# Attention on half arrays: probability-times-value and projection matmuls split into two 64-row matmuls, and the second pair's projection started in query block 4

## The reference, cut to what matters

```python
q, k, v = split(x @ c_attn_kernel.T + c_attn_bias)         # 16 heads of 64
w = softmax(q @ k.T / 8, causal)                           # per head
x = layernorm(x + (w @ v) @ c_proj_kernel.T + c_proj_bias)
h = gelu(x @ w1 + b1)                                      # 4096 wide
x = layernorm(x + h @ w2 + b2)
```

## Time and profile before

| | us |
|---|---|
| median of 3 runs | 2371.99 (2371.93 to 2372.07) |
| the profiled execution, its own time | 2373.32 |
| its span on the slowest core (core 5) | 2371.7 |
| spans of all cores | 2354.2 to 2371.7 |
| mean granted TensorE clock of the cores | 0.986 to 0.993 |

### The profile page before, as it was taken

How to read it: one execution, slowest core, us unless ns; L and a number is a source line. 1 busy time by engine, 2 the same in 40 slices (tenths; PEclk the granted TensorE clock), 3 DMA queues, 4 the chain that set the end, 5 groups by cost and what they waited for, 6 DMA issues and landing times.

```text
span 2371.7 us, 47143 instructions; the slowest of 8 cores (2354.2 to 2371.7 us)
## 1 busy us (share of the span) xinstructions
PE 2185.2 (92%) x20126; PEld 1328.4 (56%) x20126; DVE 774.7 (33%) x1925; ACT 1369.8 (58%) x1666; POOL 218.0 (9%) x181
## 2 busy tenths in 40 slices
PE   7997998999999989989878799999999999999997
PEld 3553654545545455445444466666666666666665
DVE  3434434344333343443412132222223322222221
ACT  2794788998999989999999222222222222222222
POOL 2000000000000000000111311111111111111110
PEclk8999999999999999999899899999999999999999
DMA  9500100001000000000392511100111111111000
GB/s 146 88 15 3 28 8 13 13 6 28 8 6 21 6 17 11 6 11 8 83 169 47 109 45 45 44 20 27 45 45 45 45 45 45 45 45 45 19 8 30
DMA packets 52554, 88.57 MB, mean 37 GB/s; under 512 B 3200, under 2 KB 35968, under 8 KB 51328
## 3 DMA queue, kind: packets, MB, share of 16 engines
q0 software_dynamic: 16784, 33.56, 9.2%
q1 hardware_dynamic: 35568, 52.00, 6.6%
HBM read 93.94 MB, written 25.17 MB: 50 GB/s over the span
## 4 chain that ended last, share of the span: by engine, by line
PE 80%; ACT 8%; DVE 8%; DMA 2%; issue 2%; POOL 0%; POOLq 0%; SPq 0%; DVEq 0%
PE ps L794 18%; PE ps L776 18%; PE ps L270 12%; PE ps L434 11%; PE ps L481 8%; ACT work L450 8%; PE ps L363 5%; PE ps L625 4%; DVE qkv L281 4%; DVE work L811 2%; PE ps L300 2%; DMA qkv<-w 1%; DVE stat L304 1%; PE ps L514 1%; PE ps L668 1%
## 5 line engine op out<-in xcount | busy, mean ns | idle before, releaser
L450 ACT ACTIVATE work<-ps,cb 128x1024 bf16<-128x1024 f32 (+3 forms) x1152 | 1123.3, 1059 | 158.8 <-PE ps L434 152.4
L784 ACT ACTIVATE work<-ps,b_s 128x256 bf16<-128x256 f32 x512 | 243.8, 476 | 794.7 <-PE ps L776 794.7
L794 PE MATMUL ps<-qkv,work 128*128 128x512 bf16 x2048 | 526.7, 380 | 21.3 <-DVE work L811 20.9
L776 PE MATMUL ps<-work,xT 128*128 128x256 bf16 x4096 | 533.2, 273 | 1.5 <-DVE work L518 1.5
L776 PEld LDWEIGHTS ps<-work,xT 128*128 128x128 bf16 x4096 | 401.9, 98 | 158.3 <-issue 2.3
L481 PEld LDWEIGHTS ps<-qkv,work 128*128 128x128 bf16 x8448 | 395.0, 98 | 157.1 <-issue 34.0
L434 PE MATMUL ps<-qkv 64*128 64x512 bf16 (+3 forms) x2304 | 432.2, 370 | 42.4 <-ACT work L450 37.7
L481 PE MATMUL ps<-qkv,work 128*128 128x65 bf16 x8448 | 440.9, 194 | 3.0 <-DVE work L500 2.2
L270 PE MATMUL ps<-xT,work 128*128 128x512 bf16 x1024 | 340.3, 386 | 54.5 <-DVE qkv L281 50.2
L794 PEld LDWEIGHTS ps<-qkv,work 128*128 128x128 bf16 x2048 | 198.3, 98 | 209.7 <-issue 31.1
L270 PEld LDWEIGHTS ps<-xT,work 128*128 128x128 bf16 x1024 | 79.5, 97 | 210.8 <-issue 197.6
(11 more groups left out here) (42 smaller groups left out, 744.4 us busy)
## 6 DMA issues: line engine op xcount, KB each, us to landing
work<-x SPq DMA_DIRECT2D x16, 1024.0 KB, 5.1
out<-work SPq DMA_DIRECT2D x16, 1024.0 KB, 4.0
attn_s<-work SPq DMA_DIRECT2D x64, 128.0 KB, 1.7
xT<-w POOLq DMA_DIRECT2D x8, 1024.0 KB, 14.9
work<-attn_s SPq DMA_DIRECT2D x16, 512.0 KB, 6.3
qkv<-w POOLq DMA_DIRECT2D x16, 512.0 KB, 9.3
xT<-xb POOLq DMA_DIRECT2D x7, 1024.0 KB, 45.5
work<-wqk POOLq DMA_DIRECT2D x7, 512.0 KB, 6.1
```

The costliest lines, as they stand in the source:

```text
L450: lambda: sc.activation(pb, ps, AF.Exp, bias=cb[:, 8 * p + g : 8 * p + g + 1], scale=0.125),
L776: r = t.matmul(bank(4 + ui % 2)[:, 0:TB], w1[:, FF * f + 128 * hc : FF * f + 128 * hc + 128], x2T[b % 2][:, TB * f : TB * f + TB], start=f ...
L784: lambda: sc.activation(hbuf[ui % 4], bank(4 + ui % 2)[:, 0:TB], AF.Gelu, bias=b1[:, hc : hc + 1]),
L794: r = t.matmul(bank(2 * c + oh), hbuf[ui % 4][:, 128 * c : 128 * c + 128], w2[hc][:, 512 * oh : 512 * oh + 512], start=hc == 0, stop=hc == 31)
```

## The change

1. `put_values` becomes `put_half`, run twice for a unit. The first takes rows 0 to 63 (keys) for one head and rows 64 to 127 for the other, alternating, with bank 6 and 7 each written from one half of the array. The second takes the other rows for each head ("exchanged"). So 8 matmuls of 128 rows become 16 of 64 rows. `run_halves` puts the first half before the next scores and the second behind them; the second waits on TensorE's own semaphore for the first. Where nothing stands between, halves are held back (`order[1]`).
2. The fill projections for pairs 1 to 7 become `qk_pairs` and `v_pairs`: 16 steps of two 64-row matmuls, one to bank 4 and one to bank 5, rows exchanged after step 7, so that query and key block (or two value tiles) are computed at once. Step 8 waits for step 7; `run_fill` stops after step 7. Pair 0's own projections stay as they were.
3. Costs get `GAP = 3.0` credits before a group and before the two norm sums, which now run together (`norm_pair`).
4. Pair 1's projections start in block 4 of pair 0: one block of them in `g = 4`, one in 5, two in 6, four in 7. The rate is the sum of costs over `4g + 3` units.
5. `turn_block` is held back while banks 4 and 5 are open.

```diff
+    def two_tiles(lhs0, rhs0, out0, lhs1, rhs1, out1, start, stop, after, mark):
+        def go():
+            x = t.matmul(out0, lhs0, rhs0, start=start, stop=stop, skip_group_check=True)
+            y = t.matmul(out1, lhs1, rhs1, start=start, stop=stop, skip_group_check=True)
+            return x, y
+        return pe.put(go, *after, mark=mark)
+
+    def qk_pairs(p, g):
...
+                turned, fc = divmod(n, 8)
...
+                qi0, qi1 = (1, 0) if turned else (0, 1)
...
+                tok = two_tiles(
+                    w[0:64, o0 : o0 + 128], xT[0:64, xs], bank(4 + qi0),
+                    w[64:128, o1 : o1 + 128], xT[64:128, xs], bank(4 + qi1),
+                    n == 0, n == 15,
+                    (gb_free[0], gb_free[1], ld_qk[p], ld_x[g]) if n == 0 else (st.get(7),) if n == 8 else (),
+                    n in (7, 15))
...
+        return [(1.0 + (GAP if n == 0 else 0.0), step(n)) for n in range(16)]
+
+    def norm_pair(p, g):
...
+        return [(3.0 + GAP, go)]
+
+    def v_pairs(vp, a):
...
+        return [(0.5 + (GAP if n == 0 else 0.0), step(n)) for n in range(16)]
+
+    def next_qk(p, lo, hi):
+        out = []
+        for g in range(lo, hi):
+            out += qk_pairs(p, g) + norm_pair(p, g)
+        return out
...
+    def run_halves():
+        while halves and (halves[0][1] or order[1]):
+            i, first = halves.popleft()
+            if not first:
+                order[0] = 1 - order[0]
+            put_half(i, order[0], first)
+            order[1] = False
...
-            for h in range(2):
-                o = 260 * j + 65 * (2 * (p % 2) + h)
-                for c in range(max(0, j - 4 * g), 4):
+            for c in range(max(0, j - 4 * g), 4):
+                for half in range(2):
+                    h = half ^ swap
+                    o = 260 * j + 65 * (2 * (p % 2) + h)
+                    rows = slice(64 * half, 64 * half + 64)
                     r = t.matmul(bank(6 + h)[:, 65 * c : 65 * c + 65],
-                                 pbuf[i % NP][:, 512 * h + 128 * c : 512 * h + 128 * c + 128],
-                                 w[:, o : o + 65], start=j == 0 and c == 0, stop=j == 4 * g + c,
-                                 skip_group_check=True)
+                                 pbuf[i % NP][rows, 512 * h + 128 * c : 512 * h + 128 * c + 128],
+                                 w[rows, o : o + 65], start=first and j == 0 and c == 0,
+                                 stop=not first and j == 4 * g + c, skip_group_check=True)
...
-            go()
+            order[1] = True
+            if go() and not all_:
+                break
...
-                    rate[0] = 34.0 / (4 * g + 3)
-                else:
-                    fill.extend(next_steps(0))
-                    rate[0] = sum(c for c, _ in fill) / 28.0
+                lo, hi = {4: (0, 1), 5: (1, 2), 6: (2, 4), 7: (4, 8)}.get(g, (0, 0))
+                fill.extend(next_qk(1, lo, hi))
+                rate[0] = sum(c for c, _ in fill) / (4 * g + 3)
...
-        if p == 0 and g == NG - 1 and j == 28:
-            run_fill(all_=True)
+        run_halves()
...
             put_scores(i + 1)
         t_p[i] = put_exp(i)
+        run_halves()
...
-            put_values(waiting.popleft())
+            queue_values(waiting.popleft())
...
-        while turns and i - turns[0][0] >= 5:
+        while turns and i - turns[0][0] >= 5 and not gb_open[0] and not gb_open[1]:
```

More of the change, by code:

```diff
@@ L23 @@
 NP = 7
+GAP = 3.0
 NB = S // TB
@@ L252, in build_nc @@
     sq_free = [None, None]
+    t_sq = [None, None]
     sq_next = [0]
@@ L398, in qkv0, with step, go @@
         return work
+    def two_tiles(lhs0, rhs0, out0, lhs1, rhs1, out1, start, stop, after, mark):
[5 more added lines that the diff above has]
+    def qk_pairs(p, g):
+        w = wqk[p % 2]
+        st = {}
+        def step(n):
+            def go():
+                turned, fc = divmod(n, 8)
+                if n == 0:
+                    gb_open[0] = gb_open[1] = True
+                qi0, qi1 = (1, 0) if turned else (0, 1)
+                o0 = 1024 * qi0 + 128 * fc
+                o1 = 1024 * qi1 + 128 * fc
+                xs = slice(S * fc + QB * g, S * fc + QB * g + QB)
+                tok = two_tiles(
[4 more added lines that the diff above has]
+                    n in (7, 15))
+                st[n] = tok
+                if n == 15:
+                    for qi in range(2):
+                        dst = (q2, k2)[qi][p % 2][:, QB * g : QB * g + QB]
+                        gb_free[qi] = t_qk[p, qi, g] = dve.put(
+                            lambda qi=qi, dst=dst: v.tensor_scalar(
+                                dst, bank(4 + qi), bqk[:, 8 * qi + p : 8 * qi + p + 1], None, ALU.add),
+                            tok, ld_bqk, q2_done.get(p - 2))
+                    for qi in range(2):
+                        src = (q2, k2)[qi][p % 2][:, QB * g : QB * g + QB]
+                        t_sq[qi] = dve.put(lambda qi=qi, src=src: v.tensor_mul(sq[qi], src, src),
+                                           t_qk[p, qi, g], sq_free[qi])
+                    wqk_done[p] = tok
+                    gb_open[0] = gb_open[1] = False
+                return n == 7
+            return go
+        return [(1.0 + (GAP if n == 0 else 0.0), step(n)) for n in range(16)]
@@ new lines, in norm_pair, with go @@
+    def norm_pair(p, g):
+        def go():
+            for qi in range(2):
+                tok = pe.put(lambda qi=qi: t.matmul(bank(4 + qi), ones, sq[qi], start=True, stop=True),
+                             t_sq[qi], t_ones, gb_free[qi])
+                sq_free[qi] = tok
+                c = 16 * p + 8 * qi + g
+                gb_free[qi] = t_rd[p, qi, g] = dve.put(
+                    lambda qi=qi, c=c: v.reduce_max(stat[:, c : c + 1], bank(4 + qi), axis=AX.X), tok)
+            bound(p, g)
+        return [(3.0 + GAP, go)]
@@ new lines, in v_pairs, with step, go @@
+    def v_pairs(vp, a):
+        w = wv[vp % 2]
+        st = {}
+        def step(n):
+            def go():
+                turned, fc = divmod(n, 8)
+                if n == 0:
+                    gb_open[0] = gb_open[1] = True
+                b0, b1 = (1, 0) if turned else (0, 1)
+                c0, c1 = (S * fc + 128 * (a + b0), S * fc + 128 * (a + b1))
+                ws = slice(256 * fc, 256 * fc + 256)
+                tok = two_tiles(
+                    xT[0:64, c0 : c0 + 128], w[0:64, ws], bank(4 + b0)[:, 0:256],
+                    xT[64:128, c1 : c1 + 128], w[64:128, ws], bank(4 + b1)[:, 0:256],
+                    n == 0, n == 15,
+                    (gb_free[0], gb_free[1], ld_v[vp], ld_x[a // 4]) if n == 0 else (st.get(7),) if n == 8 else (),
+                    n in (7, 15))
+                st[n] = tok
+                if n == 15:
+                    for b in range(2):
+                        gb_free[b] = t_v[vp, a + b] = dve.put(
+                            lambda b=b: v.tensor_tensor(
+                                va[vp % 2].rearrange("p (a h c) -> p a h c", a=NKT, h=4)[:, a + b, :, 0:64],
+                                bank(4 + b)[:, 0:256].rearrange("p (h c) -> p h c", h=4),
+                                bvb[:, 256 * vp : 256 * vp + 256].rearrange("p (h c) -> p h c", h=4),
+                                ALU.add),
+                            tok, ld_bv, va_done.get(vp - 2))
+                    wv_done[vp] = tok
+                    gb_open[0] = gb_open[1] = False
+                return n == 7
+            return go
+        return [(0.5 + (GAP if n == 0 else 0.0), step(n)) for n in range(16)]
@@ L400, in next_steps @@
+    def next_qk(p, lo, hi):
[3 more added lines that the diff above has]
+        return out
     def next_steps(p):
+        tiles = {1: (1, 0, 32), 2: (2, 0, 16), 3: (2, 16, 32), 4: (3, 0, 16), 5: (3, 16, 32)}
         out = []
-        if p + 1 < NPAIR:
-            out += joined([qk_block(p + 1, g) for g in range(NG)])
-        tiles = {1: (1, 0, 32), 2: (2, 0, 16), 3: (2, 16, 32), 4: (3, 0, 16), 5: (3, 16, 32)}
         if p in tiles:
@@ L407, in next_steps @@
             vp, lo, hi = tiles[p]
-            vs = [s for a in range(lo, hi) for s in v_steps(vp, a)]
-            out = vs + out
+            for a in range(lo, hi, 2):
+                out += v_pairs(vp, a)
+        if p + 1 < NPAIR:
+            out += next_qk(p + 1, 0, NG)
         return out
@@ L468, in build_nc, with queue_values, put_half @@
     attN_free = [None] * 2
-    def put_values(i):
+    halves = deque()
+    order = [0, False]
+    first_half = {}
+    def queue_values(i):
+        halves.extend([(i, True), (i, False)])
+    def run_halves():
[5 more added lines that the diff above has]
+            order[1] = False
+    def put_half(i, swap, first):
         p, g, j = units[i]
@@ L744, in build_nc @@
         while waiting and i - waiting[0] >= hold:
-            put_values(waiting.popleft())
+            queue_values(waiting.popleft())
```

(10 more changed lines are left out.)

7 lines of the change are left out of this document (6 added, 1 removed).

## The result

The changed kernel is slower: its median is 2388.36 us, against 2371.99 before. Two of its five executions fell in the chip's slow state (2614 and 2622 us), so the ratio is of the undisturbed executions alone: 1.0053, with a 95% interval of 1.0037 to 1.0069. The forecast was 2317 with a range up to 2355, so it was wrong in sign.

A forecast was written before the change was run, and what follows sets the result against it. Exponentials on ScalarE were taken to bound pairs 6 and 7, TensorE the others. Pairs 2 to 5 -36, pair 1 -12, pair 0 -5, pair 6 -0.5: -53.5, called -55, from 2372 to 2317 us; range 2272 to 2355.

The forecast's parts named there:

- What bounds the kernel: Attention: exponentials on ScalarE bound pairs 6 and 7, TensorE decides elsewhere; only time above 141 us per pair can be won.
- Price of a side-by-side pair of short matmuls: Values in halves: two 65-column matmuls side by side taken at 0.036 us, bounds 0.029 to 0.058.
- no overlap: Rival: short value matmuls don't overlap, 0.058 us per pair, +106 us, 2478; chance 0.16, whole or in part.
- the rule that the prediction cites beside it: Value halves: some 60 cycles overhead per matmul, so sixteen short matmuls would take eight's time once more.
- The wait between the halves: Each unit: second value half waits for the first behind the next scores; 0.09 us left open, bounds 0 and 0.2.
- Load per unit: TensorE in attention: 0.62 us per unit against 0.66, up to 0.07 of waits less; with fill 0.84, 0.94, 1.04.
- From load to time: Pair times from load: a tenth of a microsecond worth 12 to 16 us per pair, below about 0.9 nothing.
- Transposes may come some units later, and nobody waits for them: Attention: stores follow transposes that may come some units later, and nobody waits for them inside attention.
- Pairs 6 and 7 at "-0.5" and "0": Pair 6, already at the exponentials' bound, would change by -0.5 us, and pair 7 by 0.
- Evictions and gaps: Fill: gaps of three credits, over a microsecond, take away most waits of 5.7 + 1.7 + 1.4 + 1.2 us.
- Pair 0 (-5): Pair 0: block 7 -32 us, blocks 4 to 6 +6, +6.5, +9.5, blocks 1 to 3 +5; in sum -5.
- Given back: Rival: pair gains eaten by pair 0's packed blocks and TensorE's stalls on its own semaphore (0.2); about 2370, chance 0.07.

The follow-up runs named there:

- both edits: Changed kernel with transposes put ahead of the fill and values whole (128 rows) in pair 7; 2360.52 us, ratio to before 0.9939.
- credit by width: Changed kernel with transposes ahead of fill, pair 7 values whole, and pairs 1 to 7 credit following each unit's exponential width; 2351.09 us, ratio to before 0.9897.
- all four edits: Changed kernel with transposes ahead of fill, values whole in pairs 7 and 0, credit by the width of the unit; 2341.37 us, ratio to before 0.9857.
- The early start alone: Kernel before, with only pair 1's projections (128 rows as before) begun in block 4 of pair 0; 2365.26 us, ratio 0.9964.
- late loads: Changed kernel with feed-forward weights loaded from block 7 of pair 7, not its start; blocks 0 to 6 took 110.5 us, total 2425 us.

## Why the prediction was wrong, point by point

- **What bounds the kernel:** right. Pairs 6 and 7 are held by the exponentials (137 of 141), the others by TensorE.
- **Price of a side-by-side pair of short matmuls:** taken as 0.036, measured 0.031, near the lower bound. The rival "no overlap" is out. Nor does the trace agree, for 65 columns in two row halves, with the rule that the prediction cites beside it (Trainium skill, TensorEngine Tiling (Array Packing), Instruction Overhead), if the overhead is counted once for each matmul: sixteen of 64 rows take 0.42 us, eight of 128 rows took 0.41.
- **The wait between the halves:** 0.10 against 0.09. Right.
- **Load per unit:** forecast 0.62 + fill; with two steps 1.00 (0.57 + 0.43). Better than forecast.
- **From load to time, the step that failed.** I read the time of a pair off its mean load, from three points of one planner. The change has another planner. Its gaps are credits in which nothing runs, so the 16 steps of a group come at 2.09 per unit and not at the mean of 1.57: in pairs 2 and 3 of the kernel with both edits units with two and three steps take 1.00 and 1.21 us (medians), and those in the gaps need 0.57 and wait for ScalarE until 0.99, with only one unit of buffer between. The pairs of that kernel differ accordingly: pair 6, at 1.45 credits per unit, takes 141.5 to 145.4, pairs 2 to 5, at 2.09, take 150 with a mean load of 0.57 + 0.32 = 0.89, which had given 141.1 in the kernel before (0.88, pair 6). The run with credit by width brought them to 147 to 150 without taking work away; the run with shorter gaps made them longer, because the gaps do cover evictions. In the mean of the eight cores each of pairs 2 to 5 missed the forecast of 144.5 by 7.4 us (151.9). The transposes took 1.6 of them (150.3 with them moved) and the spreading of the steps 2 to 3 (147.5 with all four edits); what holds the rest was not taken apart.
- **"Transposes may come some units later, and nobody waits for them":** wrong, and the second failed step. Nobody waits for their result, but they wait, at the head of TensorE's queue, and the scores stand behind them: 35 us of waits, 13 us of time. I had counted what the change delays, and not what it now stands behind.
- **Pairs 6 and 7 at "-0.5" and "0":** the third failed step. I costed the added instructions by their time on the engine and found it hidden. What I had not priced is that a stream with more instructions stands still while weights load. In pair 7 that is 8 to 13 us. Pair 6 is another matter. It lost 7 to 9 us, some 4 of them to the transposes (144 with them moved, in the middle of the cores), and with all four edits it takes 139.7 to 142.5; whole values in pair 7 did nothing for it (149.0).
- **Evictions and gaps ("take away most of the waits"):** wrong in size. In pair 2 TensorE waited 10 us for VectorE, still 9.7 in the changed kernel, and 7.7 with both edits. In pair 1 the waits grew from 12.5 to 17.7 us.
- **Pair 0 (-5):** the terms were near (block 7 -27.5 for -32, blocks 4 to 6 +23 for +22, blocks 1 to 3 +2.7 for +5), the sum -1.5. The halves bought nothing there: without them blocks 1 to 3 are 5 us shorter. The early start alone gave -7.6.
- **The rivals.** None came. "Given back" (2370, chance 0.07) has the sizes of pairs 1 to 5 nearly right, but by luck: its stalls of TensorE on its own semaphore were 0.10 and not 0.2, pair 0 did not lose 10 us, and pairs 6 and 7 were not in it. The "no overlap" of the short matmuls was not what made the kernel slower.

What stays open: pair 1, which was forecast at 157 and takes 167 to 176 in all kernels with 64-row fill and 169 before. By its costs the steps of its 32 value tiles and its projections come at 2.72 per unit, denser than in pairs 2 to 5, and TensorE's waits for VectorE grew there, as said; but shorter gaps didn't shorten it (169.5), and no run took it apart further. On two of the eight cores of the kernel with both edits a hole without a semaphore (1.8 and 3.7 us) stands in it; these end 1.4 to 1.5 us after an instruction packet too, in a stretch with a DMA share of 0.66, but no run took that load away. The part of the clock is open too: late loads brought pair 7's to 0.90 and the whole loss back, so it is a small part there; what the short spells at the lower level in pairs 2 to 6 cost was not measured by itself.

## What to carry to other kernels

When two engines are matched within a tenth, as here, a cheaper unit may be worth little until the planner spreads the work: compare the densest unit with the bound, not the mean, and give filler by the slack of each unit. When an instruction is held back for a resource, look at what it waits for at the moment it is let go and who stands behind it. Use smaller and more numerous instructions only where TensorE is the bound: where it is not, as in pair 7, they bought nothing and came late under heavy DMA traffic. And read the eight cores, not one: they differ by several microseconds in a pair.

## What had not been expected of the hardware

Matmuls of 64 rows and 65 columns in the two row halves overlap almost wholly, 0.031 us for two with their weight loads. TensorE's stream can stand still for up to 6.0 us without a semaphore while weights load at 233 GB/s, and doesn't when the same loads are taken away or the stream has fewer instructions; each such hole ends just over a microsecond after a 16384-byte packet of the instruction queue has landed. The two row forms only pay together: halves with 128-row fill cost 4.0%, 64-row fill with whole values win nothing, both together take 0.10 us from a unit.
